# A batch-0 rearrangement in an RWKV attention and MoE kernel: key products interleaved by chunk, key weights by row halves, mixes and key low halves on three engines

## What is computed

```python
shifted = jnp.pad(hidden, ((0, 0), (1, 0), (0, 0)))[:, :-1]
key   = hidden * time_mix_key        + shifted * (1.0 - time_mix_key)
value = hidden * time_mix_value      + shifted * (1.0 - time_mix_value)
rec   = hidden * time_mix_receptance + shifted * (1.0 - time_mix_receptance)
k, v, r = key @ Wk, value @ Wv, jax.nn.sigmoid(rec @ Wr)
rwkv = _wkv(time_decay, time_first, k, v)      # a recurrence over the 512 tokens
return r * rwkv @ Wo
```

## Time and profile before

| | us |
|---|---|
| median of three runs | 459.14 |
| the profiled execution | 459.16 |
| its span in the trace | 457.4 |
| PE busy | 444.7 (97%) |
| DVE busy | 403.4 (88%) |
| ACT busy | 356.0 (78%) |
| POOL busy | 312.6 (68%) |

### The profile page before, as it was taken

How to read it: one execution, slowest core, us unless ns; L and a number is a source line. 1 busy time by engine, 2 the same in 40 slices (tenths; PEclk the granted TensorE clock), 3 DMA queues, 4 the chain that set the end, 5 groups by cost and what they waited for, 6 DMA issues and landing times.

```text
span 457.4 us, 6679 instructions
## 1 busy us (share of the span) xinstructions
PE 444.7 (97%) x1984; PEld 340.2 (74%) x1984; DVE 403.4 (88%) x615; ACT 356.0 (78%) x798; POOL 312.6 (68%) x300
## 2 busy tenths in 40 slices
PE   8999999999999999999999999999999999999993
PEld 3444557777888888888888888888888888888761
DVE  5989989899788989999898998989898996975985
ACT  1666757877788779888788887888798887768685
POOL 2355677588658998579858697569965695653335
PEclk9999999999999999999999999999999999999999
DMA  8703230033000042001420042100520022300016
GB/s 238 225 0 119 92 92 1 1 115 93 1 1 0 2 161 92 24 0 57 142 81 0 1 138 94 47 0 24 162 83 11 1 70 94 138 1 0 0 49 229
DMA packets 20244, 30.64 MB, mean 67 GB/s; under 512 B 2032, under 2 KB 7152, under 8 KB 20208
## 3 DMA queue, kind: packets, MB, share of 16 engines
q1 hardware_dynamic: 20064, 29.95, 20.6%
q10 hardware_dynamic: 144, 0.26, 0.2%
HBM read 21.82 MB, written 8.39 MB: 66 GB/s over the span
## 4 chain that ended last, share of the span: by engine, by line
PE 78%; DVE 4%; ACT 2%; POOL 2%; issue 1%; ACTq 0%; DVEq 0%
PE PH L451 5%; PE PV L332 5%; PE PV L338 5%; PE PR L338 5%; PE PV L333 5%; PE PR L332 5%; PE PK L332 5%; PE PK L338 5%; PE PR L333 5%; PE PK L333 5%; PE PP L361 5%; PE PP L362 4%; PE PP L366 4%; PE PT L433 3%; PE PP L381 2%
## 5 line engine op out<-in xcount | busy, mean ns | idle before, releaser
L594 ACT ACTIVATE PR<-PR 128x512 f32<-128x512 f32 x128 | 74.5, 582 | 29.7 <-PE PR L338 10.5
L1231 POOL TENSOR_TENSOR DQ<-DEN,EX 128x512 f32<-128x512 f32 x32 | 41.4, 1292 | 20.5 <-DVE DEN L890 20.5
L1237 POOL TENSOR_SCALAR NM<-SUM,RS 128x1 f32<-128x1 f32 x30 | 8.0, 268 | 62.0 <-ACT RS L594 62.0
L332 PE MATMUL PK<-KH,WKH 128*128 128x512 f32 x112 | 46.2, 413 | 0.6 <-DVE NUM L907 0.6
L944 DVE SCALAR_TENSOR_TENSOR KT<-D,VEC,XT 128x512 f32<-128x512 f32 x57 | 45.9, 853 | 0.0
L332 PE MATMUL PV<-VH,WVH 128*128 128x512 f32 x112 | 45.6, 407 | 0.0
L338 PE MATMUL PR<-RL,WRH 128*128 128x512 f32 x112 | 44.1, 394 | 0.7 <-POOL RL L1199 0.7
L332 PE MATMUL PR<-RH,WRH 128*128 128x512 f32 x112 | 44.6, 398 | 0.2 <-DVE RW L931 0.2
L338 PE MATMUL PV<-VL,WVH 128*128 128x512 f32 x112 | 43.9, 392 | 0.0
L338 PE MATMUL PK<-KL,WKH 128*128 128x512 f32 x112 | 43.9, 392 | 0.0
L333 PE MATMUL PK<-KH,WKL 128*128 128x512 f32 x112 | 43.8, 391 | 0.0
(11 more groups left out here) (281 smaller groups left out, 1285.5 us busy)
## 6 DMA issues: line engine op xcount, KB each, us to landing
XT<-in_xt SPq DMA_DIRECT2D x32, 256.0 KB, 3.5
XN<-in_x SPq DMA_DIRECT2D x28, 256.0 KB, 2.6
out<-XN SPq DMA_DIRECT2D x28, 256.0 KB, 2.0
X1T<-in_wo SPq DMA_DIRECT2D x1, 1024.0 KB, 5.3
XT<-in_x SPq DMA_DIRECT2D x4, 256.0 KB, 3.2
out<-XT SPq DMA_DIRECT2D x3, 256.0 KB, 2.3
X1T<-in_wk SPq DMA_DIRECT2D x2, 256.0 KB, 4.8
XN<-in_wv SPq DMA_DIRECT2D x2, 256.0 KB, 5.6
```

The costliest lines, as they stand in the source:

```text
L332: eng.matmul(dst[:, :], wh[:, c, o], high[:, c, :], start=(c == 0), stop=False)
L594: eng.activation(*a, **k).then_inc(q[s], 1)
L1231: eng.tensor_tensor(DQ[:, :], DEN[:, 0:T], EX[:, 1, :], ALU.add).then_inc(q["e"], 1)
```

## The change

- Loads: VEC is issued by ACT's queue ahead of its table load, no longer by SP. The key weights' columns 0 to 256 come as two row halves (chunks 0 and 1, then chunks 2 and 3, 256 KB each), between the xt chunks; the columns 256 to 512 as before.
- PE: three warm-up products in place of four. `first_keys` makes key(0) and key(1) together, both products of chunk c as soon as that chunk's mix is there. The wait for the low key weights is by block.
- ACT: four copies of the shifted x scaled by 1 - mix (OMK) for the key mixes, and four of D scaled by the receptance factor.
- DVE: OMK; the four key mixes of batch 0 are x * factor + ACT's copy, without D; no subtractions; batch 0's receptance mixes are gone. M and lead of slot 1 move ahead of slot 0's DEN. WKL is gone.
- POOL: all four subtractions of batch 0, four additions for the receptance mixes, and WKL in four blocks of 128x512, two in slot 0 ahead of batch 1's subtractions, two in slot 1 behind the value weights' low halves.
- `mixed` maps batch, kind and chunk to the count of the mixes' semaphore, in which batch 0's receptance mixes (now `r0`) are no longer counted.

```diff
@@ sync @@
-            eng.dma_start(VEC[:, :, :], vec).then_inc(q["vec"], 16)
             load_xt(0, 0)
+            load_rows(X1T, wk, "ws00", 0)
             load_xt(0, 1)
-            load_w(X1T, wk, "ws00", 0, 128)
             load_xt(0, 2)
+            load_rows(X1T, wk, "ws01", 2)
             load_xt(0, 3)
@@ sync, load_xt @@
-                if b:
-                    eng.wait_ge(q["kt"], 3 * C * (b - 1) + 2 * C + c + 1)
+                if b == 1:
+                    eng.wait_ge(q["kt"], mixed(0, 1, c))
+                    eng.wait_ge(q["r0"], c + 1)
@@ tensor @@
+            def first_keys():
+                for c in range(C):
+                    if c % 2 == 0:
+                        eng.wait_ge(q[f"ws0{c // 2}"], 16)
+                    eng.wait_ge(q["kt"], c + 1)
+                    for u in range(2):
+                        last = eng.matmul(PK[u][:, :], X1T[:, c, 128 * u:128 * u + 128], full(0, 0, c),
+                                          start=(c == 0), stop=(c == C - 1))
-            for _ in range(4):
-                eng.matmul(PP[:, :], RW[:, 0, 0:128], RW[:, 0, :], start=True, stop=True)
-            key(0)
-            key(1)
+            for n in (T, T, T):
+                eng.matmul(PP[:, 0:n], RW[:, 0, 0:128], RW[:, 0, 0:n], start=True, stop=True)
+            first_keys()
             value(0)
@@ scalar @@
+            eng.dma_start(VEC[:, :, :], vec).then_inc(q["vec"], 16)
             eng.preload_act_table_set(TABLES)
...
+            eng.wait_ge(q["om"], 1)
+            eng.wait_ge(q["cm"], 1)
+            for c in range(C):
+                eng.wait_ge(q[f"xt{c}"], 16)
+                act("y", full(0, 0, c), XT[:, c, 0:T], ACT.Copy, scale=OMK[:, c:c + 1])
+            for c in range(C):
+                eng.wait_ge(q["d"], c + 1)
+                act("rm", full(0, 2, c), D[:, c, :], ACT.Copy, scale=VEC[:, 4, c:c + 1])
             decay_gates(0)
@@ vector @@
+            def first_mix(c):
+                eng.wait_ge(q[f"xt{c}"], 16)
+                eng.wait_ge(q["y"], c + 1)
+                eng.scalar_tensor_tensor(out=full(0, 0, c), in0=XT[:, c, 1:T + 1], scalar=VEC[:, 2, c:c + 1],
+                                         in1=full(0, 0, c), op0=ALU.mult, op1=ALU.add).then_inc(q["kt"], 1)
...
-            difference(1)
-            mixes(0, 0, 0, 1)
-            difference(3)
-            mixes(0, 0, 2, 3)
+            for c in range(C):
+                first_mix(c)
             mixes(0, 1, 0, 1)
             scan_max(0)
             lead(0)
             mixes(0, 1, 2, 3)
-            mixes(0, 2, 0, 1, 2, 3)
+            scan_max(1)
+            lead(1)
             for s in SLOTS:
...
-                if s < U - 1:
+                if 0 < s < U - 1:
                     scan_max(s + 1)
                     lead(s + 1)
...
-                if s < 2:
-                    low_weights(2 * s)
@@ gpsimd @@
-            difference(0, 0)
-            difference(0, 2)
+            for c in range(C):
+                difference(0, c)
+            for c in range(C):
+                eng.wait_ge(q["rm"], c + 1)
+                eng.tensor_tensor(full(0, 2, c), full(0, 2, c), XT[:, c, 0:T], ALU.add).then_inc(q["r0"], 1)
...
+                if s == 0:
+                    low_weights(0, 0, 1)
                 if j == 0 and batch(b + 1):
                     for c in range(C):
                         difference(b + 1, c)
                 if s == 1:
                     low_weights(1, *range(C))
+                    low_weights(0, 2, 3)
```

More of the change, by code:

```diff
@@ L49, in rwkv_moe_postln @@
         VEC = sb("VEC", [128, 5, C])
-        CST = sb("CST", [128, 4, C])
+        CST = sb("CST", [128, 5, C])
         XT = sb("XT", [128, C, T + 1])
@@ L86, in rwkv_moe_postln @@
         UPT = KT[:, 1, :]
-        TD, NTD, CC, QB = (CST[:, i, :] for i in range(4))
+        TD, NTD, CC, QB, OMK = (CST[:, i, :] for i in range(5))
         def full(b, which, c):
@@ L196, in half_at, with mixed @@
             return C - 1 - c if b % 2 else c
+        def mixed(b, which, c):
+            return C * (3 * b + which) + c + 1 - (C if b else 0)
         def halved(t):
@@ L231, in load_xt @@
             def load_xt(b, c):
-                if b:
-                    eng.wait_ge(q["kt"], 3 * C * (b - 1) + 2 * C + c + 1)
+                if b == 1:
+                    eng.wait_ge(q["kt"], mixed(0, 1, c))
+                    eng.wait_ge(q["r0"], c + 1)
+                elif b:
+                    eng.wait_ge(q["kt"], mixed(b - 1, 2, c))
                 eng.dma_start(XT[:, c, 1:T + 1], xt[b, 128 * c:128 * c + 128, :]).then_inc(q[f"xt{c}"], 16)
@@ L237, in load_xn @@
                 if b == LAST:
-                    eng.wait_ge(q["kt"], 3 * C * NB)
+                    eng.wait_ge(q["kt"], mixed(LAST, 2, C - 1))
                     eng.dma_start(XT[:, n, 1:T + 1], x[b, 128 * n:128 * n + 128, :]).then_inc(q[f"xt{n}"], 16)
@@ L251, in store, with load_rows @@
                 eng.dma_start(out[b, 128 * n:128 * n + 128, :], xn_at(NT * b + n)).then_inc(q[f"out{n}"], 16)
+            def load_rows(dst, src, s, first):
+                eng.dma_start(dst[:, first:first + 2, 0:256],
+                              src.rearrange("(c p) n -> p c n", p=128)[:, first:first + 2, 0:256]).then_inc(q[s], 16)
             def load_w(dst, src, s, lo=0, hi=H):
@@ L255, in load_w @@
                    .then_inc(q[s], 16)
-            eng.dma_start(VEC[:, :, :], vec).then_inc(q["vec"], 16)
             load_xt(0, 0)
+            load_rows(X1T, wk, "ws00", 0)
             load_xt(0, 1)
-            load_w(X1T, wk, "ws00", 0, 128)
             load_xt(0, 2)
+            load_rows(X1T, wk, "ws01", 2)
             load_xt(0, 3)
             for i, (lo, hi) in enumerate(((0, 128), (128, 256), (256, H))):
-                if i:
+                if i == 2:
                     load_w(X1T, wk, f"ws0{i}", lo, hi)
@@ L270, in _ @@
             eng.dma_start(TRI[:, :], tri).then_inc(q["tri"], 16)
-            eng.wait_ge(q["lwk"], 2)
+            eng.wait_ge(q["lwk"], C)
             eng.wait_ge(q["k"], C)
@@ L311, in _ @@
         def _(eng):
+            def first_keys():
[6 more added lines that the diff above has]
+                                          start=(c == 0), stop=(c == C - 1))
+                        if c == C - 1:
+                            last.then_inc(q["k"], 1)
             def whole(dst, stage, u, which):
@@ L316, in whole @@
                     if u == 0:
-                        eng.wait_ge(q["kt"], C * which + c + 1)
+                        eng.wait_ge(q[("kt", "kt", "r0")[which]], c + 1 + (C if which == 1 else 0))
                     last = eng.matmul(dst[:, :], stage[:, c, o], full(0, which, c), start=(c == 0), stop=(c == C - 1))
@@ L327, in split @@
                     eng.wait_ge(q["hw"], which + 1)
-                    eng.wait_ge(q[("lwk", "lwv", "lwr")[which]], j + 1 if which else 2)
+                    eng.wait_ge(q[("lwk", "lwv", "lwr")[which]], j + 1)
                 for c in range(C):
@@ L633, in highs @@
                 for c in chunks:
-                    eng.wait_ge(q["kt"], C * (3 * b + which) + c + 1)
+                    eng.wait_ge(q["kt"], mixed(b, which, c))
                     if b > 1 and c < C - 1:
@@ L933, in mix @@
             def mix(b, which, c):
[L934 to L937, removed]
+                eng.wait_ge(q["d"], C * b + c + 1)
                 if b and which < 2:
@@ L1051, in _ @@
             eng.wait_ge(q["z0"], 4)
+            eng.wait_ge(q["vec"], 16)
+            eng.tensor_scalar(OMK, VEC[:, 2, :], -1.0, 1.0, ALU.mult, ALU.add).then_inc(q["om"], 1)
             eng.wait_ge(q["etd"], 1)
@@ L1253, in _ @@
                               pattern=[[-1, 128]], channel_multiplier=1).then_inc(q["idn"], 1)
-            difference(0, 0)
-            difference(0, 2)
+            for c in range(C):
[3 more added lines that the diff above has]
+                eng.tensor_tensor(full(0, 2, c), full(0, 2, c), XT[:, c, 0:T], ALU.add).then_inc(q["r0"], 1)
             def low_weights(i, *blocks):
-                stage, high, low, done = ((XN[0], WVH, WVL, "lwv"), (XN[1], WRH, WRL, "lwr"))[i - 1]
+                stage, high, low, done = ((X1T, WKH, WKL, "lwk"), (XN[0], WVH, WVL, "lwv"), (XN[1], WRH, WRL, "lwr"))[i]
                 eng.wait_ge(q["hw"], i + 1)
```

## The result

The changed kernel takes 463.47 us (463.41 to 463.71) beside 459.10 for the kernel before: a ratio of 1.0095, 95% interval 1.0081 to 1.0108. It is slower by 4.4 us, and slower than the forecast by 5.2. The profiled run of the changed kernel took 463.4 with a span of 461.6, against 457.4 before. The head of its page: busy time, share of the span, instructions.

The account below looks back on a forecast made before the run. PE was taken as the bound, with early waits on DVE's chain in slot 1; the faster front counted nothing, DEN(2) came 0.85 us earlier, so 459.16 - 0.85 = 458.3 us, range 457.5 to 459.4.

Parts of the forecast that it names:

- Nothing else in the diff touches the later part: Behind PE's early waits, all before 66 us: the whole rest only comes 0.85 us earlier.
- Keys at 5.86: Front, PE: key products start at 5.86 instead of 6.72 us, after a warm-up two passes shorter, with no wait for chunks.
- rival B: Longer front: DVE and POOL contend, or chunk 1 lands late; DEN(0) 0.5 to 1.0 later, 458.7 to 459.2; 0.21 with rival D.
- M(0) 0.2 behind key(0), and a mix at 0.66 a step: Front: key(0) ends at 11.85, M(0) starts about 0.2 later at 12.05; each DVE mix steps by 0.66 us.
- M(0) to DEN(0) 5.20: Front, DVE: four receptance mixes go, M(1) and lead(1) come; M(0) at 12.05, DEN(0) at 17.25 us.
- value(1) to value(2) 10.47: Slot 1, PE: value(1), key(2) and rec(1) need 10.47 us, from 21.94 to 32.41.
- rival D: Front: lead(1) before DEN(0) delays it by 1.9 us, value(1) at 23.2 to 23.8, gain under zero; 0.21 with rival B.
- gate(1) at 33.8: Slot 1: gate(1) follows rec(1)'s receptance pair on ACT, at 33.8 instead of 34.14 us.
- gate(1) to DEN(2) 4.10: Slot 1, DVE: mixes beside POOL cost 0.9 us more, no low weights behind them (-1.14); DEN(2) at 37.9 against 38.74.
- DEN(2) to key(5) 15.2: Slots 2 and 3: the chain behind DEN(2) is unchanged; key(5) waits for NUM(3) and starts at 53.1 us.
- Rival A: Slot 1: no contention or POOL through sooner; ACT or PE decides, gain 1.14, 457.7 to 458.0 us; chance 0.22.
- Rival C: Idle before value(1) drops PE's clock to 1.2 GHz, passes take 0.85; 459.8, or 461.6 us if held longer; chance 0.10.

Follow-up runs that it names:

- e2: Kernel before with CST widened by one unused row, moving every tile behind it 32 bytes; 462.32 us, ratio 1.0062.
- g1: Changed kernel with OMK in free bytes behind VEC, so all tiles lie where they did in the kernel before; 460.86 us, ratio 1.0040.
- g5: Same kernel as g1, run once more for its trace; 461.09 us, ratio 1.0035.
- h1: g1 without POOL's four additions, so batch 0's receptance lacks the shifted term; 459.87 us, ratio 1.0015.
- g2: g1 with the low key weights back on DVE, the changed front alone; 460.60 us, ratio 1.0028.
- g4: g1 with POOL's adds held back until the value mixes of slot 0 are done; 460.53 us, ratio 1.0025.
- g3: Kernel before with only the low key weights moved to POOL, two blocks in slot 0 and two in slot 1; 460.47 us, ratio 1.0024.
- h2: Kernel before with all low key weights on POOL in slot 0, directly behind DQ(0); 458.63 us, ratio 0.9984.
- p4: Kernel before with CST at twenty rows, moving all tiles behind it by 256 bytes; 459.23 us, ratio 0.9999.
- p1: Kernel before with 64 bytes ahead of KH and 64 more ahead of M; 461.58 us, ratio 1.0037 to 1.0067.
- e1: Changed kernel with CST at 128 bytes a partition instead of 80; 463.52 us, ratio 1.0074 to 1.0104.
- e4: Changed kernel with CST at 128 bytes and 32-byte gaps ahead of TH and X1T; 462.38 us, ratio 1.0066.
- p2: Kernel before with CST at twelve rows, moving all tiles behind it by 128 bytes; 462.06 us, ratio 1.0047 to 1.0077.
- e3: Kernel before with unused 32-byte gaps ahead of TH and ahead of X1T; 458.69 us, ratio 0.9985.

## Why the prediction was wrong

The 5.1 us between the forecast's 458.3 and the profiled 463.4 are two terms: key(5) at 55.03 in place of 53.1 (1.9), and the rest (3.1).

**"Nothing else in the diff touches the later part": failed, 3.1 us, and the larger term.** The forecast put this term at nothing. The step looked at instructions and waits, not at the allocation. e2 shows the cause with nothing else changed, and g1 and g5 take 2.4 to 2.6 us off the changed kernel by putting the tiles back (in g5 the nine groups have the sum of the kernel before; some 0.3 us more lies in the projection). The named sign, "the same spacing from there to the end", was the one that showed it. The Trainium skill, "SBUF — State Buffer", Operand start alignment, asks only for a multiple of the element size and says that this is about legality, not speed; all the addresses here are such multiples, and the runs show that speed is another matter.

**Keys at 5.86: failed by 0.58.** Two bounds, both misjudged. Chunk 0 was put ready at 5.1, as arrival, copy and mix; the copy needs OMK, OMK needs VEC, and that tiny DVE instruction was held by POOL's first subtraction and took 0.93, so the mix ended at 6.29. The wait for OMK was in the diff, and the working left it out; its length is rival B's mechanism, with an instruction that has one SBUF input. And the six warm-up passes took 4.90 us, as nearly all of them ran at the low clock level, where the sum took two passes off at 0.43. So the shorter warm-up bought nothing: in the changed kernel both ended at about the same time. The interleaving itself did what was said, with no wait between the passes.

**M(0) 0.2 behind key(0), and a mix at 0.66 a step: failed by 1.15.** This was rival B's mechanism, DVE and POOL beside each other in the front. The sum had it at nothing; in the rival it was priced at 0.3 to 0.4 a mix, 0.5 to 1.0 in all; beside an unbroken POOL a mix took 0.8 to 1.0 more. DVE's queue and not PE released M(0). h1, with the adds gone, has M(0) at 12.85, 6.28 behind its first key pass, as the forecast wanted (6.19). The forecast had let the adds "end near 14", asked only whether rec(0) would wait for them, and not what they did to DVE meanwhile.

**M(0) to DEN(0) 5.20: 5.30. DEN(0) to value(1) 4.69: 4.69. value(1) to value(2) 10.47: 10.40.** Right. So rival D, lead(1) as a delay of its own, is out, and the front is paid one for one from value(1) on. PE's idle came as 1.4 and 1.7 us in two places in place of 2 in one, which changed nothing, since DEN(0) sets value(1).

**gate(1) at 33.8: 35.68,** the 1.88 of the front and nothing else (0.58 + 1.15 + 0.10, less 0.07 of value(1) to value(2), plus 0.12 from there to the gate). **gate(1) to DEN(2) 4.10: 4.16, with +0.97 for the mixes where +0.9 was said.** Right, in size too; g2's 2.07 is the mixes without POOL. The rule on contention that was weighed there holds. Without it ACT would have released DEN(2), 1.20 behind its row of 38.14, at 39.34 and not 39.84: the slowed mixes cost the chain 0.5, not their whole 0.97. Rival B thought that a later front would spare slot 1 the contention. It did not, since POOL's queue came later too: DQ(1) hangs on DEN(1), 27.52 in place of 25.97. **DEN(2) to key(5) 15.2: 15.19.** Right.

The size was partly luck: g4 pays 1.77 for a gate 0.6 earlier, and g3 2.3.

**Rival A** needs mixes that POOL doesn't slow, and g3 has them at 1.75. **Rival C** didn't come. value(1) to value(2), right behind the longest idle time, is 10.40 for 24 passes, 0.43 each and not 0.85. The stretch of slots 0 to 3, after, has the same granted clock as the one behind it, with PE's two idle times in it (the column alone would not settle it, as it reads 1.00 over the slow passes of the start, too):

```profile
16.00:66.00 50.00, 47.09 (x128) 1.00 0.27 85
```

The slower side was thus given to the wrong mechanism. Had the two errors in the front been sized rightly, the sum would have been 459.16 - 0.85 + 1.9 = 460.2; the other 3.2 could only have come from the addresses.

## What to carry to other kernels

Before work is moved from DVE to POOL, look which DVE instructions it will run beside: here those with two SBUF inputs waited for POOL's instruction to end, and so did the one small OMK with one, so the blocks belong where DVE's instructions have an operand in PSUM (h2), not where it mixes (g3, g4). A diff that changes the size of one small tile moves every tile behind it; compare addresses before looking for another cause of a loss spread evenly over a PE-bound stretch, and put new rows where there is slack. For a new first operation, follow each of its inputs back to its own load, small vectors too.

## What the runs showed of the hardware

- **The place of tiles in SBUF and the pace of matmuls.** The nine groups of key, value and receptance passes step by 0.2296 us on average before, 0.2297 in p4, 0.2324 to 0.2327 in p1, e1 and e4, 0.2331 in p2 and 0.2335 in e2 and the changed kernel, which orders them by the place of KH. WOH with TH goes by the place of TH: 0.2351 before and in p4, 0.2299 to 0.2300 after, in e2 and in e3, where TH lies at 64. WKH to WRL, WOH and WOL, the other operands of these passes, have the same addresses in all of the kernels. Whether it is PE's reading of these tiles or another engine's traffic that depends on the place, no row shows.
- **DVE and POOL take turns.** A mix (two SBUF inputs) that began inside a POOL instruction ended 0.55 us after one of them: the earlier trace rows 35.20 and 35.76; the changed kernel 37.45 and 37.99; the value mix of its front, 10.60 with 1.76, POOL's add ending at 11.81; h1 36.60 and 37.15. One with a single SBUF input did too: OMK, four elements a partition, 0.93 us in place of 0.16, ended 0.02 to 0.03 behind POOL's subtraction in all eight runs that have it (4.67 and 4.65 in the changed one). Sometimes the next POOL instruction waits for the mix (g3: 1.72 and 1.75 in turn), sometimes it goes first (g4: 2.52). So the price is not a rate for each us of overlap, as the forecast took it, but what is left of POOL's instruction, and now and then the next one too. The Trainium skill, "GPSIMD Engine Reference", section 1, names the contention and the DVE instructions that have it, those with two SBUF inputs and those in a 2-port mode; the traces agree on the first (mixes pay, instructions with a PSUM operand do not), show no mode for the OMK instruction, and the turns and sizes are theirs.
- **The start of PE.** How long the passes of the warm-up stay at the low level (0.85 a pass) differs from run to run, also in kernels that are the same up to there: eight passes took 5.45 in the earlier trace rows and 6.51 in e2, six took 4.90 in the changed kernel, 5.49 in e4 and 4.23 in g5. Single traces of the front are thus good to some 0.4 us, and only medians decide below that.
